# Issuing each head's shifted products ahead of the next batch's score products and of the weighted values

## The reference

```python
x = x + L0_xattn(_layernorm(x), ctx, ctx)        # softmax(q k^T / sqrt(8)) v, 16 heads
x = x + L0_ffn(_layernorm(x))                    # quantised linear, conv of 3, silu, quantised linear
x = x + L1_xattn(_layernorm(x), ctx, ctx, mask)  # the same with a mask: logits + mask * -1e9
x = x + L1_ffn(_layernorm(x))                    # top 2 of 8 experts
```

## Time and profile before

| what | value |
|---|---|
| median of 3 runs | 578.35 us (575.12 to 579.55) |
| the profiled execution's own time | 579.48 us |
| its span, first to last instruction | 577.7 us |
| mean granted TensorE clock | 0.951 |
| PE busy, share of the span | 486.3 us, 84% |
| DVE | 349.5 us, 60% |
| ACT | 315.4 us, 55% |
| POOL | 201.9 us, 35% |

### The profile page before, as it was taken

The page is one execution under the profiler, slowest core; times in us unless marked ns, Lnnn a source line. Parts: engine busy times, 40 slices in busy tenths (PEclk is TensorE's granted clock), DMA queues, the critical chain, the costliest instruction groups (busy, mean ns, idle before and its releaser), DMA issues.

```text
span 577.7 us, 12491 instructions
## 1 busy us (share of the span) xinstructions
PE 486.3 (84%) x3970; PEld 404.6 (70%) x3970; DVE 349.5 (60%) x1226; ACT 315.4 (55%) x675; POOL 201.9 (35%) x429
## 2 busy tenths in 40 slices
PE   1447999899998899975799999999999897599980
PEld 1336777668776588964677877777777687599970
DVE  7886687688775146756587778678678433112203
ACT  2214776677766535553476666575566654245640
POOL 7140002221222222444211112442543657765650
PEclk9998999899999999995799999999999998789995
DMA  6314333242321992004454324234320110222107
GB/s 179 94 37 131 118 101 98 78 129 89 97 66 67 412 364 74 2 1 125 133 184 141 96 63 140 87 101 125 107 72 17 52 46 18 80 83 72 43 19 218
DMA packets 52267, 60.06 MB, mean 104 GB/s; under 512 B 7633, under 2 KB 43354, under 8 KB 50928
## 3 DMA queue, kind: packets, MB, share of 16 engines
q1 hardware_dynamic: 47248, 52.99, 29.3%
q0 software_dynamic: 2272, 4.24, 2.3%
q10 hardware_dynamic: 2688, 2.10, 1.1%
HBM read 30.01 MB, written 29.23 MB: 103 GB/s over the span
## 4 chain that ended last, share of the span: by engine, by line
PE 49%; issue 4%; DVE 4%; ACT 4%; DMA 4%; POOL 3%; SPq 1%; POOLq 0%; ACTq 0%; DVEq 0%
PE ps L1483 6%; PE ps L1536 5%; PE ps L1724 5%; PE ps L1714 5%; PE ps L1519 5%; PE ps L1539 5%; PE ps L1448 2%; PE ps L1450 2%; PE ps L1449 2%; ACT probs L901 2%; PE ps L1677 1%; PE ps L1548 1%; DMA k_blocks<-y_dram 1%; PE ps L1775 1%; DMA k_dram<-qk_parts 1%
## 5 line engine op out<-in xcount | busy, mean ns | idle before, releaser
L901 ACT ACTIVATE probs<-ps 128x512 f32<-128x512 f32 x256 | 146.7, 598 | 81.0 <-PE ps L1539 77.3
L1519 PE MATMUL ps<-k_blocks,q_stacks 128*128 128x256 f32 x512 | 119.4, 317 | 15.9 <-DVE row_max L1135 8.4
L1143 DVE CUSTOM_DVE_ANT_0 ps<-ps,mask_q 128x256 f32<-128x256 f32 x256 | 102.7, 452 | 37.5 <-PE ps L1519 36.6
L1539 PE MATMUL ps<-q_stacks,k_blocks 128*128 128x256 f32 x512 | 106.4, 292 | 1.0 <-DMA q_stacks<-maxT 0.8
L1135 DVE TENSOR_REDUCE row_max<-ps 128x2 f32<-128x512 f32 x128 | 84.3, 687 | 34.5 <-PE ps L1519 33.3
L1539 PEld LDWEIGHTS ps<-q_stacks,k_blocks 128*128 128x128 f32 x512 | 87.5, 190 | 21.0 <-issue 10.5
L1519 PEld LDWEIGHTS ps<-k_blocks,q_stacks 128*128 128x128 f32 x512 | 81.3, 197 | 22.6 <-DVE row_max L1135 12.2
L1483 PE MATMUL ps<-probs,v_aug 128*32 128x256 f32 x1024 | 69.4, 389 | 5.5 <-ACT probs L901 4.5
L763 POOL TENSOR_SCALAR max_split<-row_max 128x16 fp32r<-128x16 f32 x32 | 6.5, 204 | 182.6 <-DVE row_max L1135 79.6
L1536 PE MATMUL ps<-mask_k,neg_mask_eye 128*128 128x512 f32 x128 | 54.3, 424 | 0.4 <-DMA q_stacks<-maxT 0.4
L708 POOL DMA_INDIRECT y_dram<-x_ring x39 | 41.0, 1051 | 25.6 <-ACT x_ring L1000 19.9
(11 more groups left out here) (211 smaller groups left out, 836.7 us busy)
## 6 DMA issues: line engine op xcount, KB each, us to landing
slots_dram<-x_ring SPq DMA_DIRECT2D x1, 10400.0 KB, 29.5
q_stacks<-q_dram SPq DMA_DIRECT2D x32, 256.0 KB
q_dram<-qk_parts SPq DMA_DIRECT2D x16, 384.0 KB, 3.7
k_dram<-qk_parts SPq DMA_DIRECT2D x16, 384.0 KB, 4.0
k_blocks<-k_dram SPq DMA_DIRECT2D x128, 48.0 KB
x_ring<-slots_dram SPq DMA_DIRECT2D x39, 65.0 KB, 2.0
ctx_in<-ctx SPq DMA_DIRECT2D x16, 128.0 KB, 2.2
mask_in<-mask_Bx1xSxS_ik SPq DMA_DIRECT2D x8, 256.0 KB, 3.0
```

What stands on the lines that cost most here:

```text
L901: eng.activation(probs[:, n // HPS % 2, n % HPS, :, :].rearrange("p k q -> p (k q)"), ps[:, head_bank(BANKS_T, n)[0], :], ACT.Exp).then_in ...
L1143: last = eng.tensor_tensor_reduce(out=scored, in0=scored, in1=mask_q[1 - r][:, i, :], scale=1.0, scalar=-3.0e38, op0=ALU.add, op1=ALU.max, ...
L1519: mm = eng.matmul(ps[:, bank, i * S:(i + 1) * S], q_stack[r][:, st, i * P:(i + 1) * P], k_blocks[r][:, st, j, :], start=True, stop=True)
L1539: mm = eng.matmul(ps[:, bank, k * S:(k + 1) * S], k_blocks[r][:, st, j, k * P:(k + 1) * P], q_stack[r][:, st, :], start=(l == 0), stop=(l ...
```

## The change

In `body` of `attention_tensor` the call of T(n) moves from behind S(n) and W to the front of the slot. X(n) stays last. The order S, W, T, X becomes T, S, W, X. Nothing is added or removed, the waits stand inside the functions and move with them, and the order of no other engine changes.

```diff
                 for n in range(H):
+                    if exists(b):
+                        shifted(b, r, n)
                     if exists(b + 1):
                         scores(b + 1, 1 - r, n)
                     if n % HPS == at["pv"] % HPS:
                         if n == at["pv"] % HPS:
                             if exists(b - 1):
                                 weighted_v(eng, l, b - 1, 1 - r, 3)
                         elif exists(b):
                             weighted_v(eng, l, b, r, (n - at["pv"]) // HPS)
-                    if exists(b):
-                        shifted(b, r, n)
                     extras(b, r, n)
```

## The result

| | before | after |
|---|---|---|
| median | 576.88 us (574.06 to 579.55, 18 runs) | 582.43 us (579.39 to 584.48, 18 runs) |
| the profiled execution's own time | 579.48 us | 582.68 us |
| its span | 577.7 us | 580.9 us |
| mean granted TensorE clock | 0.951 | 0.957 |

The ratio is 1.009, with a 95% interval of 1.007 to 1.0111. That is 5.2 us slower (4.0 to 6.4). It lies inside what was called the same as well as inside the range, but the sum had said +1.6 us.

What follows compares the result with a forecast made beforehand. PE's own stream was taken to set the pace in the rounds. The six terms summed to +1.6 us, 581.1 from the profiled 579.48; put on the runs' median of 578.35, the forecast was 580.0 us, range 574.5 to 586.

Steps and rivals of the forecast that it cites:

- two of its own signs: Prediction wrong if rounds in either layer change by more than 0.4 us, or new windows with clock under 0.9 appear.
- Term 1: Layer 0, L1677: W one T later leaves ACT's copy uncovered, PE waits 0.1; 0.12 per slot, six rounds, +0.7 us.
- Term 2: Layer 0, W(13): T(13) in front fills its wait for head 11's exponential, so 0; without that cover 1.7 us.
- Term 3: Layer 0 round starts: S(0) queues behind T(0)'s wait for the maxima; free in four rounds, three starts pay, +1.4 us.
- Term 4: Layer 1, first round: T(0) waits for the maxima and S(0) of 0.34 follows, +0.3 us.
- the term of the clock: PE's joined waits, 0.5 before T(0) and 1.0 before L1602, are under 1.24 us, so no clock fall: 0.
- Term 5: Layer 1, slot 4: S(4) later, so DVE's maximum, L1157 and L1602 slip 0.30 us in four rounds, +1.2 us.
- Term 6: Last round of each layer: T before W lets ACT work during W; -1.4 us in layer 1, -0.6 in layer 0, -2.0.
- W's new neighbours: Behind W now stands X or the next T: taken as no gain or loss, bound 2.8 us either side.
- The cover is missed: Rival: each round pays for T no longer behind S(15) and S(0) behind the load; about 584 us, chance 0.14.
- The clock falls: Rival: the clock falls in the joined waits, six to ten times 1.4 us; 588 to 594 us, chance 0.10.

Runs made afterwards that it cites:

- turn_kept: The changed kernel, but slots 13, 14, 15 and 0 of layer 0's rounds, except the last, in the old order: 581.43 us, 1.0076 of before.
- slot0_kept: The changed kernel, but slot 0 of all rounds except the last, in both layers, in the old order: 583.56 us, 1.0114 of before.
- l0_only: The kernel before, with the new order in layer 0 alone: 579.97 us, 1.0059 of before.
- slot4_only: The kernel before, with T(4) ahead of S(4) in slot 4 of layer 1's rounds except the last: 578.96 us, 1.0039 of before.
- slot4_kept: The changed kernel, but slot 4 of layer 1's rounds, except the last, in the old order: 577.48 us, 1.0023 of before.
- last_only: The kernel before, with T first only in the last round of each layer: 575.30 us, 0.9982 of before; measured again, 574.93 us, 0.9966.
- s_t_w: The changed kernel, but with T between S and W in every slot (order S, T, W, X): 577.06 us, 0.9994 of before.
- last_and_13: The kernel before, with T first in the last rounds and S, T, W in slot 13 of layer 0's other rounds: 575.14 us, 0.9962 of before.

## Why the prediction was right or wrong

The verdict "within 1%" and the range held. The size didn't: the sum said +1.6 us and the runs say +5.2 (4.0 to 6.4). The same sum on the traces gives 2.4 - 0.6 in layer 0 and 1.7 + 2.2 - 1.2 in layer 1, +4.5 us, of which 1.6 are the fall of the clock at layer 1's start, which the order alone doesn't bring. With a change of 0.9%, "within 1%" held by a tenth of a per cent, which is luck as much as forecast. By two of its own signs the prediction was wrong: round 2 of layer 0 and round 5 of layer 1 grew by more than 0.4 us (0.52 and 0.45), and a new window with a clock under 0.9 appeared, 0.74 at layer 1's start.

- **Term 1, the copy of the raw output, +0.7: right.** The mechanism is exact. L1677 starts 1.86 us after W(1) (131.47 - 129.61 in the rows above); I had written 1.87. It comes 0.35 behind S(2), at 131.12, where it came 0.23 behind T(2): the wait of 0.1. The slot ends up 0.07 later where I said 0.12, +0.4 over six rounds.
- **Term 2, W(13), 0: wrong, +1.2.** The failed step is "T(13), moved in front of it, fills that wait". I proved that W(13) waits for the exponential of head 11, and did not ask how long. The row has a wait of 0.25, in the other rounds it is 0.16 in the mean, and T(13) takes 0.34. A wait hides only its own length. In the seven rounds X(11) to W(13) is longer by 0.13 to 0.23, in sum 1.25 us. I had the price of the lost cover in the text (1.7) and gave it no share. `turn_kept` gives back 0.18 here.
- **Term 3, the start of a round, +1.4: right in the four steady rounds, too large in the others.** From W(13) to X(0) it is the same before and after in rounds 3 to 6 (3.83 in the rows shown), T(0) waits 0.72 for a landing that takes 1.92 us from issue to release (the second of the two loads at 125.25 begins 0.55 later, and T(0) is at 127.72; I took 1.85), and POOL still lets X(0) go. `slot0_kept` undoes the move and gains nothing there. At 107 us, the end of round 2, the move costs 0.22, which `slot0_kept` gives back; I had put 0.5. At 70 us, the end of round 0, what is left over the other rounds' cost is 0.4 - 0.24, and in front of X(0) of round 0 it is 0.4; both are less than the spread between kernels of one order. Together that is some 0.8 us against 1.4.
- **Layer 0 in sum.** Terms 1 to 3 said 2.1 and the rounds show 2.4, through another distribution: that they agree is luck, a missed 1.2 against two terms that were too large. Less the end's 0.6 the traces give +1.8, or +2.2 with the stretch in front of the ruler, and `l0_only` measures 3.4 us (2.0 to 4.8). So 1.2 to 1.6 us of layer 0 are in the median of the runs and not in the ruler of one trace.
- **Term 4, the first round of layer 1, +0.3: wrong where the clock falls.** After shows +2.2. The fall is 1.6 of it, and T(4) in round 0 is 0.2 (`slot4_only`). `slot4_kept` and `turn_kept`, which have the same order at the start and no fall, show +0.4 and +1.0, and the old order itself varies by 1.0. The failed step is "both are under 1.24, so 0" in the term of the clock. The wait that the new order joins at this place was not among the two that I looked at. It was in my own rows in part: 0.38 stood in front of T(0), and the trace has 0.80 in front of S(0), which the new order joins to it. With the 0.34 of the S(0) that no longer stands between, the three make 1.5 us; after has 1.89.
- **Term 5, the product v, +1.2: right in place and mechanism, too small in size.** DVE waits for S(4), S(4) is late by T(4), L1602 slips, and all of PE behind it. The rounds 1 to 6 show 0.22, 0.33, 0.38, 0.35, 0.45 and 0.01, in sum 1.7. I had 4 x 0.30. A round that pays costs 0.35 in the mean and not 0.30, and there are five of them and not four (rounds 1 to 5); round 0 pays 0.2 more. PE's wait is 4.3 us against the 3.2 that I had named.
- **Term 6, the last rounds, -2.0: right.** -0.6 and -1.2 by the marks against -0.6 and -1.4; ACT's waits for T fell by 2.4 and 1.8 us; `last_only` runs 0.9982 and 0.9966.
- **W's new neighbours, 0: right.** `s_t_w` has T in front of each W and X or the next S behind, and its rounds are the old ones to 0.1 us in layer 1.
- **The rivals.** "The cover is missed" (about 584) came nearest in time, but not in cause: it let each round of layer 0 pay for the T that stands behind S(15), and what was paid is a T in front of W(13). "The clock falls" was right once, at a place that I had not put on its list, and not in the rounds of layer 0. In 108 to 112 us, behind a wait of 1.26 us in front of T(0), after ran at full clock where the earlier trace rows had 0.58:

```profile
108.00:112.00 4.00, 2.74 (x31) 1.82 (x29) 2.49 (x4) 1.84 (x4) 2.19 (x6) 1.00 0.48 154
```

From the Trainium skill ("TensorE: Matmul & The Clock Gate", section "HAM oscillation — how this bites in real kernels") I had drawn a fall in every round of layer 0. That was a wrong use of it: the waits in that section's loop are of 3 to 5 us. Here T(0) waits 0.7 to 1.7 us in six rounds of after, and the clock holds behind all of them, so these traces don't contradict the section. What they show beside it is a few falls behind waits of under 2 us.

What stays open is what makes the clock fall at layer 1's start in three executions and not in those of `slot4_kept` and `turn_kept`, where PE idled as long, and how often it falls in the runs without a profile. Open too is the part of layer 0's +3.4 us that no round shows, and why `s_t_w` doesn't reach the time of `last_only` though its rounds and ends are as good; the two intervals overlap.

## What to carry to other kernels

In a software pipeline that is bound by one engine, ask of each product who waits for it: here S feeds the longer chain (DVE, POOL, the loads, the product v), so each T put in front of it costs up to its own length wherever nothing else waits longer at the chain's end, and one such slot of sixteen (slot 4) made 2.2 us by itself. A wait found in the trace hides work only up to its own length, so read its mean over the rounds before a moved instruction is put into it at no cost. Where the feeding stage is absent, as in the last round, the same move gains: T first in the last rounds only is the simplest of the best versions here, 575.30 and 574.93 us, 0.9982 (0.9962 to 1.0001) and 0.9966 (0.9943 to 0.9989) of the kernel before.

## What was not expected of the hardware

The granted clock fell behind waits of PE of 1.33 and 0.18 us with an S between the earlier trace rows, of 1.24 and 0.24, of 1.76, of 1.81 and 0.16 (`last_and_13`), of 1.89 and of 2.22 us (`slot0_kept`). It held behind waits of 1.19 and 0.28 us (`last_only`), 1.26, 1.91 and 2.00 us, and even 2.77 us (`s_t_w`, at 71.80). So the length of the last wait alone doesn't decide it, within 1.2 to 2.8 us, and no order of mine steered it. At the start of layer 0, behind 2.91 us in front of T(0) in after, it was low too, as it was there in each of the thirteen traces, whatever the order.

A fall in the rounds cost 1.4 to 1.6 us where it came, as much as the whole gain of the last rounds. The kernel before has one in its profiled execution, and kernels with the same rounds lack it at that place. I had found no cause for the 1.1 us by which that execution lay above its median. This fall and the late load in front of it, 2.5 us together, are a likely one, which no run shows.

The loads vary as much. At one place in one order, S(0) at about 70 us, PE waited 0.76 us for k in before and 1.69 in `slot4_only`.
